# Attention on one core: a new order of ScalarE's and VectorE's work in a unit, score and output matmuls of 128 columns, weights of a head requested one head ahead

## What is computed

```python
q = rope((x @ Wq).reshape(b, n, H, HD))
k = rope((x @ Wk).reshape(b, n, H, HD))
v = (x @ Wv).reshape(b, n, H, HD)
k_cmp, v_cmp = means of k and v over blocks of 64 tokens
p_cmp = softmax(q @ k_cmp.T * scale, masked)
p_slc = softmax(q @ k.T * scale, causal and in the 8 best blocks)
p_swa = softmax(q @ k.T * scale, causal and at most 64 tokens back)
o = g_cmp * (p_cmp @ v_cmp) + g_slc * (p_slc @ v) + g_swa * (p_swa @ v)
out = o.reshape(b, n, H * HD) @ Wo
```

## Time and profile before

| | us |
|---|---|
| median of 3 runs | 2613.45 |
| lowest and highest | 2612.63, 2614.03 |
| the profiled execution | 2615.07 |
| its span, first to last instruction | 2613.2 |

### The profile page before, as it was taken

One profiled execution on the slowest core, in us unless ns is written; L12 is line 12 of the kernel. 1 busy time (PEld: TensorE's weight loads), 2 busy tenths in 40 slices (PEclk: granted clock), 3 DMA queues, 4 the chain that ended last, 5 costly groups with the idle time before them and its releaser, 6 DMA issues. The chain is left out here.

```text
span 2613.2 us, 48889 instructions
## 1 busy us (share of the span) xinstructions
PE 2488.2 (95%) x12944; PEld 2065.2 (79%) x12944; DVE 1840.7 (70%) x6021; ACT 1413.8 (54%) x3938; POOL 1598.5 (61%) x1177
## 2 busy tenths in 40 slices
PE   4799999999999999999999999999996999999998
PEld 3688888888888888888888888888885888887776
DVE  6387878787878787878777777777774466566134
ACT  6556666666666656565666666666663222222442
POOL 0377777676767777777777777777772434333442
PEclk9899999999999999999999999999997999999999
DMA  3122212121212222222221212121213443342356
GB/s 118 52 56 65 69 51 70 50 71 49 72 48 72 60 60 60 60 60 60 60 71 49 72 48 72 49 71 49 70 50 140 154 144 112 128 145 69 97 172 214
DMA packets 145629, 211.74 MB, mean 81 GB/s; under 512 B 14912, under 2 KB 56128, under 8 KB 144576
## 3 DMA queue, kind: packets, MB, share of 16 engines
q1 hardware_dynamic: 145600, 211.37, 27.3%
HBM read 93.87 MB, written 50.33 MB: 55 GB/s over the span
## 5 line engine op out<-in xcount | busy, mean ns | idle before, releaser
L463 PE MATMUL bank<-xt_hi,w_hi 128*128 (+1 forms) x1536 | 613.0, 399 | 4.5 <-DVE causal_h L728 3.7
L463 PE MATMUL bank<-xt_lo,w_hi 128*128 (+1 forms) x1536 | 601.2, 391 | 0.0
L463 PE MATMUL bank<-xt_hi,w_lo 128*128 (+1 forms) x1536 | 600.6, 391 | 0.0
L436 POOL TENSOR_TENSOR qk_lo<-s_full,qk_hi 128x512 fp32r<-128x512 f32 x256 | 330.4, 1293 | 257.9 <-ACT qk_hi L556 257.6
L424 POOL TENSOR_TENSOR cosed<-s_full,rope 128x512 f32<-128x512 f32 x256 | 329.1, 1289 | 178.3 <-ACT s_full L545 178.2
L432 POOL TENSOR_TENSOR s_full<-cosed,s_swap 128x512 f32<-128x512 f32 x256 | 329.4, 1287 | 36.7
L463 PEld LDWEIGHTS bank<-xt_hi,w_lo 128*128 128x128 f32 x1536 | 289.1, 188 | 63.2
L463 PEld LDWEIGHTS bank<-xt_hi,w_hi 128*128 128x128 f32 x1536 | 289.3, 188 | 58.1 <-DVE causal_h L728 4.0
L571 ACT ACTIVATE bank<-bank,shift 128x512 f32<-128x512 f32 (+3 forms) x512 | 262.4, 512 | 134.2 <-DVE bank L631 134.2
L463 PEld LDWEIGHTS bank<-xt_lo,w_hi 128*128 128x128 f32 x1536 | 289.7, 189 | 52.1
L429 POOL TENSOR_TENSOR s_swap<-s_swap,rope 128x512 f32<-128x512 f32 x256 | 330.4, 1291 | 0.0
(11 more groups left out here) (170 smaller groups left out, 5831.4 us busy)
## 6 DMA issues: line engine op xcount, KB each, us to landing
s_swap<-s_full SPq DMA_DIRECT2D x512, 128.0 KB, 2.3
o_scratch<-o_sb SPq DMA_DIRECT2D x128, 256.0 KB, 2.0
o_raw<-o_scratch SPq DMA_DIRECT2D x32, 1024.0 KB, 6.2
xin<-in_L_attn_x SPq DMA_DIRECT2D x16, 1024.0 KB, 5.3
w_raw<-in_L_ffn_W SPq DMA_DIRECT2D x64, 256.0 KB, 3.2
base_scratch<-x SPq DMA_DIRECT2D x8, 1024.0 KB, 4.7
base<-base_scratch SPq DMA_DIRECT2D x32, 256.0 KB, 4.2
out<-base SPq DMA_DIRECT2D x32, 256.0 KB, 2.7
```

What stands on the lines that cost most here:

```text
L436: nc.gpsimd.tensor_tensor(qk_lo[k][:], s_full[k][:], f32(qk_hi[k][:]), ALU.subtract).then_inc(lo_done[k], 1)
L463: last = nc.tensor.matmul(banks[QB[k]][:, :], w[k][:, c, :], v[:, bass.ds(b, 1), c, :], start=(n == 0), stop=(n == 3 * C - 1))
```

## The change

Six edits, all in `attend` and in `Weights.load`:

1. ACT: `qk_hi` of q goes ahead of the exponentials of row 3, that of k behind those of row 2; then rows 1, the compressed scores, and row 0; `vt` and `o_sb` come behind them.
2. DVE: the mix of row 1 goes ahead of `v_lo`.
3. PE: score row 0 and key block 3 of the output have 128 columns; the buffers `pt_hi` and `pt_lo` lose the 128 zero columns, and one copy of 384 columns takes the place of 256 and 128.
4. The two memsets of the zero columns go, and PE waits for the other three constants at its first scores, not at its start.
5. SP: the loads of head h + 1 stand behind the second unit of the loop over head h (for head 1, behind unit 1), with a loop written for SP alone.
6. `Weights.load` waits for the raw buffers in every head but the first.

```diff
--- before.py
+++ after.py
@@ -29,8 +29,8 @@
 E1OFF = [0, 128, 384, 768]
 E1W = 1280
 PTOFF = [0, 512, 896, 1152]
-PTQ0 = [0, 128, 256, 256]
-PTW = 1408
+PTQ0 = [0, 128, 256, 384]
+PTW = 1280
 
 
 def consts():
@@ -125,7 +125,7 @@
 
     def load(self, sp, h):
         for k in range(3):
-            if not isinstance(h, int):
+            if not (isinstance(h, int) and h == 0):
                 sp.wait_ge(self.split[k], h * 2)
             sp.dma_start(self.raw[k][:], self.dram[k][:, :, bass.ds(h * HD, HD)]).then_inc(self.loaded[k], 16)
 
@@ -372,8 +372,6 @@
     def steps(eng, body, start=lambda h: None, spare=lambda: None):
 
 
-
-
         start(0)
         body(0, 0, True, False, False, False)
         body(1, 1, True, True, False, False)
@@ -398,9 +396,7 @@
                 sp.dma_start(s_swap[k][0:64, :], s_full[k][64:128, :]).then_inc(swapped[k], 16)
                 sp.dma_start(s_swap[k][64:128, :], s_full[k][0:64, :]).then_inc(swapped[k], 16)
 
-            def body(u, b, project, score, end, split):
-                if split is not False:
-                    weights.load(sp, split)
+            def body(u, b, project, score, end):
                 if project:
                     swap(u, 0)
                     swap(u, 1)
@@ -414,7 +410,27 @@
                 sp.wait_ge(projected[2], H * B)
                 chunks.load_first(sp, 0)
 
-            steps(sp, body, spare=load_chunks)
+            def head_from_second(first, second, h):
+
+                body(first, B - 1, True, True, True)
+                body(second, 0, True, True, True)
+                if not (isinstance(h, int) and h == H - 1):
+                    weights.load(sp, h + 1)
+                with sp.Fori(1, B - 1) as b:
+                    body(h * B + b, b, True, True, True)
+
+            body(0, 0, True, False, False)
+            body(1, 1, True, True, False)
+            weights.load(sp, 1)
+            with sp.Fori(2, B - 1) as b:
+                body(b, b, True, True, True)
+            with sp.Fori(1, H - 1) as h:
+                head_from_second(h * B - 1, h * B, h)
+            head_from_second((H - 1) * B - 1, (H - 1) * B, H - 1)
+            body(H * B - 1, B - 1, True, True, True)
+            body(H * B, None, False, True, True)
+            load_chunks()
+            body(H * B + 1, None, False, False, True)
             sp.wait_ge(out_slot_free, 16 + 16 * H * B)
 
         @block.gpsimd
@@ -476,10 +492,12 @@
                     project_one(b, 1)
                 if score:
 
+                    if not end:
+                        pe.wait_ge(zeros_set, 3)
                     pe.wait_ge(lo_done[0], u)
                     pe.wait_ge(lo_done[1], u)
                     for t in SCORED:
-                        w = max(256, (t + 1) * P)
+                        w = (t + 1) * P
                         if end:
 
                             pe.wait_ge(probs_ready, (u - 2) * T + mixed_at[t])
@@ -532,7 +550,6 @@
             def start(h):
                 head[0] = h
 
-            pe.wait_ge(zeros_set, 5)
             steps(pe, body, start)
 
         @block.scalar
@@ -558,11 +575,7 @@
             def pt_high(u, g):
                 w = (512, 384, 384)[g]
                 act.wait_ge(pt_ready, (u - 2) * 3 + g + 1)
-                if g < 2:
-                    nc.scalar.activation(pt_hi[:, PTOFF[g]:PTOFF[g] + w], banks[6 + g][:, 0:w], ACT.Copy).then_inc(pt_hi_done, 1)
-                else:
-                    nc.scalar.activation(pt_hi[:, PTOFF[2]:PTOFF[2] + 256], banks[4][:, 0:256], ACT.Copy)
-                    nc.scalar.activation(pt_hi[:, PTW - P:PTW], banks[4][:, 256:384], ACT.Copy).then_inc(pt_hi_done, 1)
+                nc.scalar.activation(pt_hi[:, PTOFF[g]:PTOFF[g] + w], banks[(6, 7, 4)[g]][:, 0:w], ACT.Copy).then_inc(pt_hi_done, 1)
 
             def exp_of_row(u, t):
 
@@ -586,30 +599,30 @@
                 if end:
                     for g in range(3):
                         pt_high(u, g)
+                if project:
+                    high(u, 0)
                 if score:
                     for t in (3, 2):
                         exp_of_row(u, t)
                         exp_of_window(u, t)
                 if project:
-                    high(u, 0)
+                    high(u, 1)
+                if score:
+                    exp_of_row(u, 1)
+                    exp_of_window(u, 1)
+                    act.wait_ge(cmp_step, (u - 1) * NC + 3)
+                    nc.scalar.activation(sc, sc, ACT.Exp).then_inc(exp_cmp, 1)
+                    exp_of_row(u, 0)
+                    exp_of_window(u, 0)
+                if project:
                     if score:
                         act.wait_ge(v_transposed, u)
                     evacuate(u, 2)
-                if score:
-                    exp_of_row(u, 1)
-                    exp_of_window(u, 1)
                 if end:
                     act.wait_ge(out_ready, u - 1)
                     act.wait_ge(out_slot_free, (u - 2) * 16 + 16)
                     nc.scalar.activation(o_sb[:], banks[6][:, :], ACT.Copy).then_inc(out_evacuated, 1)
-                if project:
-                    high(u, 1)
                 if score:
-
-                    act.wait_ge(cmp_step, (u - 1) * NC + 3)
-                    nc.scalar.activation(sc, sc, ACT.Exp).then_inc(exp_cmp, 1)
-                    exp_of_row(u, 0)
-                    exp_of_window(u, 0)
                     act.wait_ge(v_transposed, u)
                     nc.scalar.activation(v_hi[:].rearrange("p t d -> p (t d)"), banks[7][:, :], ACT.Copy).then_inc(v_hi_done, 1)
                 if split is not False:
@@ -633,14 +646,8 @@
             def pt_low(u, g):
                 w = (512, 384, 384)[g]
                 dve.wait_ge(pt_hi_done, (u - 2) * 3 + g + 1)
-                if g < 2:
-                    nc.vector.tensor_tensor(pt_lo[:, PTOFF[g]:PTOFF[g] + w], banks[6 + g][:, 0:w],
-                                            f32(pt_hi[:, PTOFF[g]:PTOFF[g] + w]), ALU.subtract).then_inc(pt_lo_done, 1)
-                else:
-                    nc.vector.tensor_tensor(pt_lo[:, PTOFF[2]:PTOFF[2] + 256], banks[4][:, 0:256],
-                                            f32(pt_hi[:, PTOFF[2]:PTOFF[2] + 256]), ALU.subtract)
-                    nc.vector.tensor_tensor(pt_lo[:, PTW - P:PTW], banks[4][:, 256:384],
-                                            f32(pt_hi[:, PTW - P:PTW]), ALU.subtract).then_inc(pt_lo_done, 1)
+                nc.vector.tensor_tensor(pt_lo[:, PTOFF[g]:PTOFF[g] + w], banks[(6, 7, 4)[g]][:, 0:w],
+                                        f32(pt_hi[:, PTOFF[g]:PTOFF[g] + w]), ALU.subtract).then_inc(pt_lo_done, 1)
 
             def mix(t, part, to):
 
@@ -716,17 +723,15 @@
                     mix_far(1)
                     mix_window(v, 2)
                     mix_near(1)
+                    mix_window(v, 1)
                     dve.wait_ge(v_hi_done, v + 1)
                     nc.vector.tensor_tensor(v_lo[:].rearrange("p t d -> p (t d)"), banks[7][:, :],
                                             f32(v_hi[:].rearrange("p t d -> p (t d)")), ALU.subtract).then_inc(v_lo_done, 1)
-                    mix_window(v, 1)
-
-            nc.vector.memset(f32(pt_hi[:, PTOFF[3]:PTOFF[3] + P]), 0.0).then_inc(zeros_set, 1)
-            nc.vector.memset(f32(pt_lo[:, PTOFF[3]:PTOFF[3] + P]), 0.0).then_inc(zeros_set, 1)
+
             nc.vector.memset(sc, 0.0).then_inc(zeros_set, 1)
             nc.vector.tensor_copy(ident_h[:], m("ident")).then_inc(zeros_set, 1)
             nc.vector.tensor_copy(causal_h[:], m("causal")).then_inc(zeros_set, 1)
-            dve.wait_ge(zeros_set, 5)
+            dve.wait_ge(zeros_set, 3)
             steps(dve, body, spare=lambda: chunks.low_wo(dve, 0))
```

## The result

| | before | changed |
|---|---|---|
| median, us | 2613.74 (4 runs) | 2596.59 (4 runs, 2593.68 to 2596.75) |
| span of the profiled execution, us | 2613.2 | 2594.8 |
| mean granted clock of PE | 0.987 | 0.981 |

The ratio is 0.9931 [0.9919, 0.9943]: faster by 17 us, a third of the forecast 52, outside the range from 2540 to 2592. So the gain is sure, and the question is where the other 35 us went.

The account below looks back on a forecast made before the run. ACT's order was taken to delay DVE, stalling PE 0.48 us a unit. Stall -60.5, short matmuls -3.8, new waits +12 make -52.3 us; from the 2613.45 us median that gives 2561 us, range 2540 to 2592.

Parts of the forecast that it names:

- The swap alone would not bring this ... PE would wait at the transposes instead: DVE's new order alone, row 1 ahead of `v_lo`, would not bring the 60.5 us, DVE's loop being as long as before.
- vt is what is late next: On ACT, `vt` for PE's k projection becomes the next tight point, margin about 1.0 us; two units per head can use it up.
- 1: Rival: short 128-column matmuls run at the plain float32 rate, price 81.4 us, 2646 us, slower than before; chance 0.12.
- 3: Rival: in 128-column matmuls the columns are paid, in full gaining 45 us instead of 3.8, 2520 us; chance 0.08.
- its milder form: 128-column matmuls take about 81 ns each in a stream with weight loads, giving 2537 us; no separate chance given.
- 4: Rival: ACT's chain isn't shortened, compressed scores being late for line 610; DVE stays the bound, near 2610 us; chance 0.02.
- 2: Rival: PE's stall moves to the k projection, 0.3 us in each of 128 units, 38 us, 2600 us; chance 0.10.
- The sum for ordinary units: PE's stall gone, 126 x 0.48 = 60.5 us, plus six short matmuls a unit at 0.112 us, 3.8 us.
- What comes new: New PE waits in a head's last and second units, 15 x 0.8 = 12 us against; bounds nothing and 26 us.
- The margin is about 1.0 us.: In an ordinary unit ACT ends `vt` about 1.0 us before PE needs it for the next unit's k projection.
- Late by up to 1.5 + 0.9 = 2.4 us, part of it hidden ... I take 0.5.: Second unit's swap behind the load: 1.5 us for issues, 0.9 for shared DMA; PE loses 0 to 1.4 us, 0.5 taken.
- under 1 us once, not counted: At the start, two memsets and PE's early wait go, a gain of under 1 us once, left out of the sum.

Follow-up runs that it names:

- kernels 8 and 9: 8: kernel 2 with DVE's order undone, 2556.70 us; 9: kernel before with only the new ACT and DVE orders, load and padding as they were, 2611.71 us.
- kernel 7: Kernel before with DVE's order alone changed, the mix of row 1 ahead of `v_lo`: 2601.68 us, ratio to before 0.9954.
- kernel 2: Changed kernel with the weight loads issued behind the swaps of a head's second unit, not ahead of them: 2556.50 us, ratio to before 0.9779.
- kernel 4: Kernel 2 with each load split, 1 of 128 partitions ahead of the second unit's swaps and 127 behind: 3059.60 us, ratio to before 1.1711.
- kernel 10: Changed kernel with the padding to 256 columns put back (score row 0, key block 3): 2596.09 us, ratio to before 0.9929.

## Why the prediction was wrong

**Right.** *What bounds the kernel:* ACT's order, then DVE, then PE's 0.48 us; taken away by ACT's order (kernels 8 and 9), DVE's loop then has about 1.0 us to spare (it waits 0.37 for scores and 0.62 for `pt_hi`). *"The swap alone would not bring this ... PE would wait at the transposes instead":* so it was (kernel 7), though 12 us came of it and not none. *"vt is what is late next":* it was, in just the two units per head that were named (and at the start, which was not). *The rivals:* 1 falls, and 3 with the columns paid in full (0.102 us per short matmul); its milder form holds in part: a short matmul saves 0.015 us, a quarter of the 0.059 of columns paid in full. 4 falls (0.99 us of wait), 2 falls (ordinary units have no wait). *The sum for ordinary units:* 60.5 + 3.8 = 64.3 us forecast, 71.2 measured; the 7 more are the short matmuls, taken at 0.112 us and worth 0.015 instead of 0.005 each. The 0.112 was read from plain float32 matmuls, each issued twice; it is not the floor of a float32r one.

**Wrong: the term "What comes new".** It held 12 us, with 26 as its bound; measured were 48. Three of its steps failed, the second with the largest part:

1. *"The margin is about 1.0 us."* It is 0.63, in two parts. In the changed kernel PE starts 248.49 - 247.84 = 0.65 us behind the start of `vt`, so it could go on at 1010.58 + 0.65 = 1011.23, against 1012.03 for the first matmul of the k projection (12 of 0.23 us behind the q projection's start at 1009.23): 0.80 us. I had put that at 1.0. The other part is that a stop costs more than its wait. In the second unit shown above the k projection's first matmul comes 248.49 - 246.56 - 0.23 = 1.70 us late (246.56 is the start of the matmul ahead of it), yet the unit is 1.88 longer; the first matmuls behind a stop follow each other more slowly. The "1.54" of the row is less than both. For the last unit the lateness was right (1.3 forecast, 1.25 measured), and these two things made 0.3 into 0.59; the row there shows a wait of 0.29.
2. *"Late by up to 1.5 + 0.9 = 2.4 us, part of it hidden ... I take 0.5."* The 0.9 for the bytes is the term that was mis-sized. The issue was 1.6 us late, as forecast. The second half of q's swap landed 4.3 us behind its issue instead of 2.3, which is 2.0 us and not 0.9. The hidden part was right: in kernel 2 the swapped data lie ready 1.1 us before POOL comes to them, and the 0.5 had taken 0.9 for that. So the forecast's 1.5 + 0.9 - 0.9 - 1.0 = 0.5 should have been 1.6 + 2.0 - 1.1 - 0.6 = 1.9, the 1.88 measured in the unit shown. The row for it was there: the earlier trace rows has "2.5/3.2/4.0", and the 3.2 is the median of two kinds. q's swaps, issued right behind the three loads in that kernel too, landed in 3.8 and 4.0 us; k's, issued 2.4 us after q's, in 2.5. The maximum was the one to take.
3. *PE's clock.* No step had it. A wait of 1.9 us can be followed by 1.2 GHz: six of 14 heads, 1.57 us each, 9.4 us.

With 15 x 0.59 + 14 x (2.77 - 0.63) + 6 x 1.57 = 48.2 in place of 12, the sum meets the 48. These sizes are measured in this same trace, so the sum shows that nothing is left over, not that the sizes could have been known. Which wait is followed by the low clock stays open.

**Wrong: "under 1 us once, not counted"** for the start. PE reaches the first transposes at 139.43 instead of 135.66 us, although it began the attention at 99.66 instead of 102.48: the stretch between is 6.6 us longer. Only 0.7 of the earlier beginning is PE's shorter wait for the constants (3.01 instead of 3.74 us); the kernels with the changed start began at 99.2 to 102.5 us (kernel 4 apart), so the rest lies within what they vary by. Of the 6.6, some 2.5 are again the clock: in kernel 10, with waits of the same length, it stays at 1.00 behind the second one, and the stretch is 37.3 us instead of 39.8. Units 0 and 1 have no slack: `vt` stands there behind exponentials that wait for the first rotation (changed kernel, PE's timeline):

```profile
115.59 0.47 PE L479 MATMUL bank<-xt_hi,w_hi 128*128 128x512 f32 x1 [2.13 <-ACT vt L562]
...
131.68 0.77 PE L479 MATMUL bank<-xt_hi,w_hi 128*128 x1 [3.19 <-ACT vt L562]
```

The order was read in the steady unit only.

## What to carry to other kernels

A new order that takes an engine's chain off the bound makes some other chain the tight one; write down its margin, and hold every irregular unit (first, last, the one with an extra load) against it separately. Where a view gives a minimum, a median and a maximum over few transfers, ask which of them is the one that will be waited for. Put bulk transfers *behind* the small ones that something waits for, on the same queue: here that single move was worth 40 us, more than twice the change itself. Where several edits come together, ask which of them is the condition for the others: the new order without the earlier load gained nothing.
